# A post-norm decoder layer on one core: scores, logits and transposes as pairs of half-height products

## The reference

```python
# 1: scores against a learned table (k, v: 1024 x 64), 4 heads of 64
q = layernorm(x, g, b) in heads; p = square(relu(q @ k.T)); out = x + p @ v
# 2: cross attention with ctx, 16 heads of 16
logits = Q @ K.T * 0.25
D = clip(frac[k] - frac[q], -0.2, 0.2)
attn = gamma*logits + delta*(ap[h]*max(D, 0) + an[h]*min(D, 0))
out = softmax(attn) @ V @ Wo.T + bo
# 3: FFN 256 -> 1024 -> 256 with relu; the top-1 expert of 8 adds a rank-4 term
```

## Time and profile before

| | |
|---|---|
| median of 3 runs | 875.0 us (874.97 to 875.61) |
| span of the profiled execution | 873.6 us |
| its own time, taken as the median: span and 1.4 us around it | 875.0 us |
| granted PE clock | full in every slice of the page |
| DMA, share of the 16 engines | 25.2% |

### The profile page before, as it was taken

How to read it: one execution, slowest core, us unless ns; L and a number is a source line. 1 busy time by engine, 2 the same in 40 slices (tenths; PEclk the granted TensorE clock), 3 DMA queues, 4 the chain that set the end, 5 groups by cost and what they waited for, 6 DMA issues and landing times.

```text
span 873.6 us, 20940 instructions
## 1 busy us (share of the span) xinstructions
PE 851.8 (98%) x7168; PEld 683.9 (78%) x7168; DVE 756.6 (87%) x2164; ACT 711.7 (81%) x1946; POOL 588.1 (67%) x758
## 2 busy tenths in 40 slices
PE   7999899999999999999999999999999999999997
PEld 6667578778778777877878787787878778788786
DVE  6888898889898898989889898988989888799964
ACT  5559898798888979888897888889888888879851
POOL 6758886768677776867777676677777677654421
PEclk9999999999999999999999999999999999999999
DMA  7223312212231221322222132222223122222200
GB/s 190 80 50 68 69 36 56 50 21 55 59 65 36 56 56 26 68 46 60 42 56 55 26 67 43 58 48 52 49 35 68 37 61 51 38 50 44 49 14 25
DMA packets 40187, 46.15 MB, mean 53 GB/s; under 512 B 10417, under 2 KB 27313, under 8 KB 40082
## 3 DMA queue, kind: packets, MB, share of 16 engines
q1 hardware_dynamic: 40082, 44.82, 25.2%
HBM read 15.42 MB, written 4.19 MB: 22 GB/s over the span
## 4 chain that ended last, share of the span: by engine, by line
PE 89%; ACT 4%; DVE 2%; SPq 2%; issue 1%; DMA 1%; POOL 0%; POOLq 0%; DVEq 0%
PE bank L300 12%; PE bank L404 12%; PE bank L253 10%; PE bank L485 10%; PE bank L417 7%; PE bank L395 7%; PE bank L288 7%; PE bank L289 6%; PE bank L373 3%; PE bank L495 2%; PE bank L354 2%; PE bank L334 2%; PE bank L379 2%; ACT P L701 1%; PE bank L320 1%
## 5 line engine op out<-in xcount | busy, mean ns | idle before, releaser
L1168 POOL TENSOR_SCALAR U<-DP,alph 128x512 f32<-128x512 f32 x256 | 192.3, 752 | 122.8 <-DVE NM L924 67.8
L701 ACT ACTIVATE P<-T,NM 128x256 f32<-128x256 f32 x512 | 256.3, 511 | 1.4 <-DVE NM L924 1.3
L1150 POOL TENSOR_TENSOR R<-R 128x512 f32<-128x512 f32 x208 | 219.2, 1054 | 44.8 <-ACT R L645 44.7
L917 DVE SCALAR_TENSOR_TENSOR bank<-DN,alph,bank 128x512 f32<-128x512 f32 x256 | 191.2, 747 | 28.5 <-PE bank L395 24.9
L924 DVE CUSTOM_DVE_ANT_0 T<-bank,U 128x256 f32<-128x256 f32 x512 | 197.0, 422 | 8.9
L621 ACT ACTIVATE STG<-bank 128x512 f32<-128x512 f32 x256 | 152.3, 595 | 38.4 <-PE bank L404 37.3
L645 ACT ACTIVATE R<-bank 128x512 f32<-128x512 f32 x248 | 146.8, 596 | 29.0 <-PE bank L289 24.4
L404 PE MATMUL bank<-ident,P 128*128 128x128 f32 x1024 | 155.6, 274 | 6.1 <-ACT STG L621 5.5
L404 PEld LDWEIGHTS bank<-ident,P 128*128 128x128 f32 x1024 | 118.3, 140 | 30.7 <-ACT P L701 14.7
L300 PE MATMUL bank<-R,VS 128*32 128x512 f32 x992 | 118.3, 593 | 0.6 <-issue 0.4
L395 PE MATMUL bank<-QS 128*128 128x256 f32 x512 | 111.8, 300 | 2.7 <-DVE NM L924 2.2
(11 more groups left out here) (184 smaller groups left out, 1886.4 us busy)
## 6 DMA issues: line engine op xcount, KB each, us to landing
QS<-QK SPq DMA_DIRECT2D x384, 64.0 KB, 2.4
XG<-in_x SPq DMA_DIRECT2D x16, 256.0 KB, 3.0
CT<-in_ctxT SPq DMA_DIRECT2D x16, 256.0 KB, 4.4
out<-XO SPq DMA_DIRECT2D x15, 256.0 KB, 2.2
FK<-in_frac SPq DMA_DIRECT2D x16, 128.0 KB, 3.3
STG<-in_wiT SPq DMA_DIRECT2D x2, 512.0 KB, 4.3
STG<-in_woT SPq DMA_DIRECT2D x2, 512.0 KB, 3.9
STG<-in_kT SPq DMA_DIRECT2D x2, 256.0 KB, 4.5
```

The source lines that it names most:

```text
L701: eng.activation(P[n % NP][:, cs], T[n % NT][:, cs], ACT.Exp, bias=NM[:, n % 8, q:q + 1], scale=-1.0, accum_out=SU[n // 16 % 2][:, q, seat ...
L917: eng.scalar_tensor_tensor(out=L[:, :], in0=dn[:, :], scalar=alph[:, 16 + h:17 + h], in1=L[:, :], op0=ALU.mult, op1=ALU.add).then_inc(s_t1, 1)
L1150: eng.tensor_tensor(r, r, r, ALU.mult).then_inc(s_sqp, 1)
L1168: eng.tensor_scalar(U[n % NU][:, :], dp[:, :], alph[:, h:h + 1], 0.0, ALU.mult, ALU.add).then_inc(s_u, 1)
```

## The change

Three products change their shape, and the rest is made to fit:

- `scores` takes both halves h of a table block at once: six matmuls of 64 rows by 512 columns, h = 0 on partitions 0 to 63 into one bank and h = 1 on 64 to 127 into another, in turn. SK now holds all high parts in one tile and all low parts in another, so `skh` and `skl` are one instruction each.
- QS holds the two heads of a pair at partitions 0 and 64, 48 rows each, so no zeros are needed; `logits` takes two heads as four matmuls of 48 rows, in turn into the two banks pL. It waits until both heads before are read out.
- `turn` takes two heads as 16 transposes of 64 rows by 128, in turn into two banks of the ring. `turned` copies each bank, a row half of both heads, into STG in runs of 64.
- pT becomes the fourth bank of the ring. T, P and STG get a buffer or two more (NT, NP 3 to 4, NQ 6 to 8). `biased` handles a pair. `head` and the order of columns of Wv and rows of Wo follow.
- Every `due` gets new instants. Steps of the paired stages go from 16 of about 39 to 8 of 68 to 78.

```diff
-        pL, pT, pV, pA = psum[3:5], psum[5], psum[6], psum[7]
+        pL, pV, pA = psum[4:6], psum[6], psum[7]
-        QS = [sb(f"QS{i}", [128, 2, 4, 256], f32r) for i in range(2)]
+        QS = [sb(f"QS{i}", [128, 2, 2, 256], f32r) for i in range(2)]
-        NU, NT, NP, NQ = 2, 3, 3, 6
+        NU, NT, NP, NQ = 2, 4, 4, 8
-        ring, used, bank_of = [0, 1, 2], {}, {}
+        ring, used, bank_of = [0, 1, 2, 3], {}, {}
...
-            def scores(b, u):
-                c, h = unit(u)
-                bank, before = take("sc", b, u)
-                bank_free(before)
+            def scores(b, c):
+                cs = slice(c * 128, c * 128 + 128)
+                banks = []
+                for h in range(2):
+                    bank, before = take("sc", b, 2 * c + h)
+                    bank_free(before)
+                    banks.append(bank)
                 pe.wait_ge(s_wlo["kT"], 1 + c // 4)
-                pe.wait_ge(s_skl, 2 * b + h + 1)
-                both = sk(b, h)
-                eng.matmul(bank[:, :], KH[:, c * 128:c * 128 + 128], both, start=True, stop=False)
-                eng.matmul(bank[:, :], KL[:, c * 128:c * 128 + 128], both, start=False, stop=True).then_inc(s_sc, 1)
+                pe.wait_ge(s_skl, b + 1)
+                for j, (k, part) in enumerate(((KH, 0), (KL, 0), (KH, 1))):
+                    for h in range(2):
+                        i = eng.matmul(banks[h][:, :], k[half(h), cs], sk(b, part)[half(h), :], start=(j == 0),
+                                       stop=(j == 2))
+                i.then_inc(s_sc, 1)
...
-            def logits(n):
-                G, L = n // 4, pL[n % 2]
+            def logits(p):
+                G, m = p // 2, p % 2
                 pe.wait_ge(d_q[G % 2], 96 * (G // 2 + 1))
-                pe.wait_ge(s_tt, 2 * (n - 1))
+                pe.wait_ge(s_tt, 4 * p)
                 for q in range(2):
-                    i = eng.matmul(L[:, q * 256:q * 256 + 256], QS[G % 2][:, 0, n % 4, q * 128:q * 128 + 128],
-                                   QS[G % 2][:, 1, n % 4, :], start=True, stop=True)
+                    for j in range(2):
+                        rows = slice(64 * j, 64 * j + 48)
+                        i = eng.matmul(pL[j][:, q * 256:q * 256 + 256], QS[G % 2][rows, 0, m, q * 128:q * 128 + 128],
+                                       QS[G % 2][rows, 1, m, :], start=True, stop=True)
...
-            def turn(n):
-                pe.wait_ge(s_ex, 2 * n + 2)
-                pe.wait_ge(s_ev, n)
-                for k in range(2):
-                    for q in range(2):
-                        i = eng.transpose(pT[:, k * 256 + q * 128:k * 256 + q * 128 + 128],
-                                          P[n % NP][:, q * 256 + k * 128:q * 256 + k * 128 + 128], ident[:, :])
+            def turn(p):
+                banks = []
+                for j in range(2):
+                    bank, before = take("turn", 0, 2 * p + j)
+                    bank_free(before)
+                    banks.append(bank)
+                pe.wait_ge(s_ex, 4 * p + 4)
+                for e in range(2):
+                    for k in range(2):
+                        for q in range(2):
+                            o = e * 256 + k * 128 + q * 64
+                            for j in range(2):
+                                i = eng.transpose(banks[j][:, o:o + 64],
+                                                  P[(2 * p + e) % NP][half(j), q * 256 + k * 128:q * 256 + k * 128 + 128],
+                                                  ident[half(j), half(j)])
...
-                for b, u in due(g, -7, 16, 39, early=4, late=7):
-                    logits(16 * b + u)
+                for b, u in due(g, -11, 8, 74, early=35, late=5):
+                    logits(8 * b + u)
-                for b, u in due(g, 114, 16, 41, late=9):
-                    turn(16 * b + u)
+                for b, u in due(g, 114, 8, 78, early=42, late=7):
+                    turn(8 * b + u)
-                for b, u in due(g, -943, 4, 143, early=14):
+                for b, u in due(g, -943, 4, 148, early=-135, late=-4):
                     av(b, u)
-                for b, u in due(g, 336, 4, 143, early=-1, late=2):
+                for b, u in due(g, 269, 4, 148, early=8, late=49):
                     values(4 * b + u)
-                for b, u in due(g, -1161, 16, 37, early=-95, late=1):
+                for b, u in due(g, -1158, 8, 73, early=-189, late=2):
                     scores(b, u)
```

More of the change, by code:

```diff
@@ L590, in _ @@
                     bias_o()
-                for b, _ in due(g, -278, early=31, late=-28):
+                for b, _ in due(g, -276, early=-126, late=40):
                     turned_over("x1T", b, X1, s_x1, 2 * b + 2, s_x1T)
-                for b, _ in due(g, -241, early=-788, late=51):
+                for b, _ in due(g, -239, early=-877, late=35):
                     kp(b)
-                for b, _ in due(g, -213, early=43, late=-18):
+                for b, _ in due(g, -223, early=-74, late=52):
@@ L596, in _ @@
                     qp(b)
-                for b, _ in due(g, -142, early=70, late=4):
+                for b, _ in due(g, -147, early=182, late=-12):
                     vp(b)
-                for b, _ in due(g, 1093, early=36, late=-46):
+                for b, _ in due(g, 1118, early=9, late=-31):
                     turned_over("x2T", b, X2, s_x2, 2 * b + 2, s_x2T)
-                for b, _ in due(g, 1189, early=8, late=-76):
+                for b, _ in due(g, 1179, early=-22, late=349):
@@ L610, in _ @@
                     xnT(0)
-                if g == -688:
+                if g == -807:
                     xnT(1)
-                for b, _ in due(g, -1221, start=2, late=1):
+                for b, _ in due(g, -1225, start=2, late=-31):
                     xnT(b)
@@ L635, in skh @@
                     act.wait_ge(s_xg, 2)
-                act.wait_ge(s_sc, 16 * b if b > 2 else 16 * (b // 2))
-                for h in range(2):
-                    own = slice(64 * h, 64 * h + 64)
-                    eng.activation(sk(b, h)[own, :], turned[own, :], ACT.Copy).then_inc(s_skh, 1)
+                act.wait_ge(s_sc, 8 * b if b > 2 else 8 * (b // 2))
+                eng.activation(sk(b, 0), turned, ACT.Copy).then_inc(s_skh, 1)
             def relu(b, u):
                 g = 16 * b + u
-                act.wait_ge(s_sc, g + 1)
+                act.wait_ge(s_sc, g // 2 + 1)
                 act.wait_ge(s_av, slot_free[g])
@@ L755, in _ @@
             for g in GRID:
[L756 removed]
+                for b, u in due(g, 1297, 4, 36, early=-7, late=476):
                     ih(b, u)
[L758 removed]
+                for b, _ in due(g, -376, early=903, late=-9):
                     x1(b)
[L760 removed]
+                for b, u in due(g, 28, 16, 38, early=27, late=6):
                     exps(16 * b + u)
[L762 removed]
+                if g == -4999:
@@ L763, in _ @@
                     skh(0)
-                if g == -578:
+                if g == -1030:
                     skh(1)
-                for b, _ in due(g, -1221, start=2, late=13):
+                for b, _ in due(g, -1260, start=2, late=-7):
                     skh(b)
-                for b, _ in due(g, -476, early=3, late=2):
+                for b, _ in due(g, -491, early=-275, late=2):
                     heads_out(b)
-                for b, u in due(g, 133, 16, 40, early=1, late=12):
-                    turned(16 * b + u)
@@ L772, in _ @@
-                for b, _ in due(g, 863, early=-51, late=19):
+                for b, u in due(g, 119, 8, 76, early=49, late=33):
+                    turned(16 * b + 2 * u)
+                    turned(16 * b + 2 * u + 1)
+                for b, _ in due(g, 820, early=-13, late=449):
                     aoh(b)
-                for b, _ in due(g, 809, early=-39, late=-8):
+                for b, _ in due(g, 774, early=-64, late=97):
                     rb(b)
-                for b, _ in due(g, 1065, early=46, late=-12):
+                for b, _ in due(g, 977, early=101, late=-53):
@@ L863, in skl @@
                     turned = XN[:, :, :].rearrange("p h t -> p (h t)")
-                for h in range(2):
-                    dve.wait_ge(s_skh, 2 * b + h + 1)
-                    own, other = slice(64 * h, 64 * h + 64), slice(64 - 64 * h, 128 - 64 * h)
-                    eng.tensor_tensor(sk(b, h)[other, :], turned[own, :], f(sk(b, h)[own, :]),
-                                      ALU.subtract).then_inc(s_skl, 1)
+                dve.wait_ge(s_skh, b + 1)
+                eng.tensor_tensor(sk(b, 1), turned, f(sk(b, 0)), ALU.subtract).then_inc(s_skl, 1)
             def square(b, u):
@@ L1103, in _ @@
                     cl(b)
-                for b, _ in due(g, -275, early=35, late=11):
+                for b, _ in due(g, -243, early=-51, late=65):
                     low("x1T", b, X1L, X1H, s_x1h, s_x1l)
```

(16 more changed lines are left out.)

330 lines of the change are left out of this document (160 added, 170 removed).

## The result

The changed kernel takes 867.1 us (864.6 to 868.7, 4 runs) against 875.3 us beside it (875.0 to 877.5, 4 runs): a ratio of 0.990, 95% interval 0.987 to 0.992. It is faster by 8 us where 34 were forecast, and lies inside the range. The profiled execution took 868.24 us with a span of 866.4, 7.2 less than the span of before.

The account below looks back on a forecast made before the run. PE was taken to bound the kernel at 51.25 us per batch; 6.9 saved by halves, less 4.2 for shape changes and 0.4 for waits, gave 49.0. 32 us over 14 batches plus 2 outside made 841 us, range 808 to 900.

Parts of the forecast that it names:

- 47.5 to 50.5: Steady batch: the forecast of 49.0 us per batch counts as wrong if the period falls outside this range.
- 36 x 0.16: PE's shape changes: 36 per batch instead of 10, at 0.16 us each, so 4.2 us more.
- the halves' 6.9: PE's saving per batch from paired half-height work: scores 1.9, logits 1.9, `turn` 3.1 us.
- the bound of 0.22 for the exit: Upper bound on one shape change's price on PE, counting the whole exit; extra changes then cost 5.7 us per batch.
- I take 0.4 per batch: Added PE waits from coarser paired steps and bank takes: 0.4 us per batch, within bounds of none to 4.4.
- 14 batches: Batches counted between `ao` of batch 0 and batch 14, at 2.3 us less each: 32 us.
- I count them as one batch more, 2 us: Fill and drain outside the steady batches: claimed to save as much as one batch more, 2 us.
- DVE's floor of 47.3: DVE per batch: 45.15 us busy plus 2.1 us idle left, so it can't go below 47.3.
- rival B: Cheap shape changes on PE, 0.10 us each, so DVE would bound: 807 us; chance 0.13.
- Rival C: Two to eight pairs' waits of 0.55 us per batch eat the gain: 852 to 901 us; chance 0.26.
- Rival E: An issue floor of 0.056 us per matmul on PE slows `turn`: period 51.9, 885 us; chance 0.04.
- F: Row halves don't run side by side on PE: period 60.0, 1006 us; chance 0.04.

Follow-up runs that it names:

- x1: Changed kernel plus one full-height filler matmul in the middle of each `turn`, eight per batch, forcing two extra shape changes each; 929.1 us, ratio 1.062.
- x2: Changed kernel plus the same eight filler matmuls per batch, placed at FFN-in where no shape changes; 893.9 us, ratio 1.022.
- x5: Changed kernel with each batch's last `turn` moved 11 instants back, behind the first FFN product; 875.2 us, ratio 0.999 to the kernel before.
- x9: Changed kernel with ACT's second adapter-input copy reading the first copy in SBUF, so DVE may use the bank sooner; 860.4 us, ratio 0.983.
- x12: The changed kernel run once more, unedited, beside later runs; 866.9 us, ratio 0.990 to the kernel before.
- x14: x9 with the sixth `scores` of a batch moved behind `turn` and `logits`, one shape change less; 873.0 us, ratio 0.996 to the kernel before.
- x15: x9 plus filler matmuls ahead of PE's waits in the fill and drain; 858.6 us, ratio 0.980 to the kernel before.
- x3: Changed kernel with `scores`' six matmuls issued as three of one half, then three of the other; 866.9 us, ratio 0.991 to the kernel before.

## Why the prediction was wrong

The mechanism of a steady batch was right: PE bounds it, halves run side by side, most of their gain goes into changes of shape, and the period came out at 49.96 where 47.5 to 50.5 was the test. Wrong were the sizes in the batch's difference and, outside the steady batches, the path that sets the time. The gain forecast was four times the gain measured, by these steps:

- **"36 x 0.16"** and the halves' 6.9. By the parts undone they are 0.17 and 6.15, which is 0.25 and 0.75 us per batch; by the starts they are 0.19 and 6.9, and all is in the changes. Either way 1.0 of the 2.3 us forecast per batch did not come. The forecast is the difference of two large terms, so a small error in each is a large one in it. How much falls on which term is not settled. I had the bound of 0.22 for the exit in the earlier trace rows and took the low figure, although a visit of half-height fp32r products looks like these rows (0.19 at each edge), and not like the 40-row transposes of the earlier trace rows. x1 and x2 show 0.16 for transposes only, x5 0.18.
- **"I take 0.4 per batch"** for waits. It is 0.46, so the size is right. It is not the pairs' logits but a bank of the ring, and not for the reason I gave: `turn` and `scores` do not crowd each other out while FFN out keeps a bank, but the small readers behind `uT` hold one for long. x9 shows that it could be had back.
- **"14 batches"** between the two `ao`. There are 13 periods: 663.5 us by 51.25 gives 12.9. A slip that a division would have shown: 2.3 us.
- **"I count them as one batch more, 2 us"** for fill and drain. This is as large a failure as the period's. Start to `ao` 2 and `ao` 13 to the end lost 6.1 us where 6.6 were to be gained. I took PE's work as the limit where chains of waits set the time: shorter PE work makes longer waits there (1.76 us at 65 us, 0.81 at the same place before). Behind such waits stood half clock, which I had not in the sum at all. x12 against the first profile prices two of those stretches (66 and 107 us) at 4.4 us. Without them the fill still gives next to nothing: `ao` 2 comes at 209.63 in x12 and at 209.99 before, and `ao` 13 to the end takes 102.7 us against 100.8.

DVE's floor of 47.3 was too high: DVE is busy for 42.9, as the pair's `biased` instructions overlap (256 of 0.749 us, 192 us, are 180.2 us busy). Only rival B's price rested on it. Rival C named the right kind of loss and its likeliest 860 to 875 holds the result, yet that is luck, as its mechanism is not what happened: one wait of 0.46 us a batch, not two to eight. Its argument against itself, that PE did not wait with DVE at 89%, was sound. Rival E's ground is gone: 16 transposes in 0.47 us are 0.029 each. The rows that speak against F are the earlier trace rows, not rows 8. The rule of about 62 ns per matmul without hardware decode, in the Trainium skill ("TensorE: Matmul & The Clock Gate", section "Wait — 56ns, not 53.3ns?"), does not describe this trace.

What stays open: how the miss of 1.0 us splits between price and gain, why the change of shape that x14 takes away gives nothing back where it was, what decides whether a given wait is followed by half clock, and the drain. From `ao` 13 to 15 it is 1.4 us longer than before even in x12, half clock at 813 to 819 us included.

The best kernels are x9 (860.4 us) and x15 (858.6 us), about 7 and 8 us below the changed kernel.

## What to carry to other kernels

When a gain is the difference of a large saving and a large price, measure the price by itself first, in the shapes it will have: eight fillers at one place and then at another did it here. A wait that a move only shifts belongs to the resource; shorten what holds it. In a fill or drain that chains of waits limit, count a faster engine as nothing. There idle time on TensorE can cost clock as well, as it did here, and differently from run to run.

## What the hardware showed that I had not expected

- TensorE starts products of two row halves out of program order (x3): three of one half, then three of the other, run as three pairs, period 50.03 against 49.96.
- At one place a half-height visit between a column-group visit and full-height work cost no more than the same visit joined to another half-height one (7.61 us in x9 and in x14).
- The same program with the same waits of 1.8 and 1.0 us kept a clock of 1.00 in one run and 0.70 over 11.5 us in another; over eight runs that spread is 864 to 869 us.
